# A Mamba scan whose chunk front is made over two chunks, with narrow products in column groups of TensorE

## The chip, the cores and the metric

The kernel runs on one core of a Trainium2 chip. The metric is the device time of one execution in microseconds, lower is better. The engines are named as in the profile: PE (TensorE matmuls) and PEld (its weight loads), DVE (VectorE), ACT (ScalarE), POOL (GpSimd), SP (the queue that issues DMAs). Each has its own instruction stream and they meet at semaphores only.

## What is computed

Two layers on x of 128 sequences, 64 steps and 256 features, all in fp32. The first is a linear attention with a FiLM output; the second, which takes three quarters of the time, is a Mamba block. Cut to what matters here, with the 64 steps in a permuted order:

```python
h  = layernorm(x) * (1 + scale) + shift              # [128, 64, 256]
xm, z = split(h @ W_in)                              # 512 features each
xm = silu(causal_conv(xm, conv_w, 4 taps) + conv_b)
dtr, B, C = split(xm @ W_xp, [64, 16, 16])
dt = softplus(dtr @ W_dt + b_dt)                     # [128, 64, 512]
for each step t, state s of 16:                      # A = -exp(A_log)
    hst = hst * exp(dt_t * A) + (dt_t * xm_t) * B_t
    y_t = sum_s(hst * C_t)
y = (y + xm * D) * silu(z)
out = x + gate * (y @ W_out)
```

## The kernel before

After the attention part and a setup the Mamba part works through CHUNKS = 16 chunks of T = 4 steps. It is written as *bodies*: body c scans chunk c. A body has 64 *slots* (ITEMS = 16 states x 4 steps), and in each slot i an engine does one item of the scan and whatever else is put in that slot. Items go in blocks of eight: four states, two steps.

One item on its way: ACT makes the decays exp(dt * A) of a whole block one block ahead, two `decay` activations (L632) in each slot; PE turns an item's four 128x128 decay tiles into one of four PSUM banks, two slots ahead (`turn_decay`, L527); DVE multiplies them by the state (`keep_state`, L742) and adds dt * x * B (`feed_state`, L752), two items at a time; POOL (L452), or ACT for the states 3, 7, 11 and 15 (L675, in slot i+2), multiplies the new state by C into one of eight `scaled` buffers; PE sums it into a y bank with transposing matmuls, LAG = 5 slots later (`sum_state`, L537). ACT's scaling waits for DVE's item, PE's turn waits for the item four before it, and each engine's stream is strictly in order.

The *front* of a chunk prepares its scan. In its order of data: rows are gathered by DMA into xg and modulated on POOL; PE turns them (jobs h0, h1, L575) and ACT copies them to hT; PE multiplies by W_in for x (u0 to u3, L579) and ACT copies the product to raw and makes the first tap of the convolution (L665); the other taps are on POOL (two of four feature blocks, L464 and L468) and DVE (two, L798); ACT takes tanh (L701) and DVE the silu product (L804); PE makes the low-rank input (job dtr, L584), dt (dt0 to dt3, L593) and B and C (bc, L589); ACT takes relu, abs and exp of dt (L654, L656, L670) and one Ln (L704) with a table load on either side; POOL adds them and multiplies by x (L475, L478); PE turns the product (x0 to x3, L597) and ACT copies it to dtx (L658). For z there are z0 to z3 (L570), a tanh (L708) and gates on POOL (L503, L507). Jobs out0 and out1 (L567) multiply the gated y of half a chunk by W_out; DVE scales the rows (L769) and SP stores them. Skip terms x * D are PE's L548, y's gate DVE's L761.

All products of the front share two PSUM banks in turn (`side_bank`): a job waits until the one before the last has been copied out. Which slot a job, tap, tanh or gate stands in is given by hand, by the table `SLOTS` and the numbers behind it. In the kernel before, body c makes the whole front of chunk c+1: h and u in slots 0 to 10, z in 14 to 21, dtr 22 to 25, dt 27 to 33, bc 35 to 38, x in 48 to 54. Body -1 makes chunk 0's front and scans nothing; body 15 scans and makes none.

## Time and profile before

| | |
|---|---|
| median of the runs | 2333.99 us (2333.95 to 2335.63) |
| profiled execution, its own time | 2334.89 us |
| its span, first to last instruction | 2333.1 us |
| PE / DVE / ACT / POOL busy over the span | 88% / 84% / 72% / 70% |
| attention part, from the start to about | 545 us |
| setup and first front, to the first item of the scan | 620.3 us |
| scan, to the last item | 2265 us |
| last rows, gather by permutation, final sum and store, to the end | 2333.1 us |

How to read it: a busy share says how much work an engine had, not who set the pace. In the scan the timelines show for each engine which instruction started when, how long it took, and in brackets how long the engine stood idle before it and whose result ended that. Consecutive instructions of a kind are merged into one row with their count; engines are pipelined, so the distance between two starts is shorter than the duration printed.

### The profile page before, as it was taken

How to read it: one execution, taken by the hardware profiler on the slowest of the kernel's cores; microseconds unless marked ns; L12 is line 12 of the kernel's file. 1: busy time of each engine (PE TensorE's matmuls, PEld its weight loads, DVE VectorE, ACT ScalarE, POOL GpSimd, SP SyncE). 2: the span in 40 equal slices, each digit the busy share in tenths (PEclk: the TensorE clock that was granted, in tenths of full speed). 3: DMA queues.
4: the chain of work that ended last, by engine and by line, in shares of the span. 5: the costliest groups of instructions: out<-in, count | busy, mean ns of one | idle time of the engine just before them, and what ended most of it. 6: DMA issues, size and time to landing. Idle time of an engine off the chain costs nothing. (4 is left out here: it accounts for less than half of the span.)

```text
span 2333.1 us, 44474 instructions
## 1 busy us (share of the span) xinstructions
PE 2051.4 (88%) x13497; PEld 1579.0 (68%) x13497; DVE 1969.4 (84%) x3686; ACT 1688.3 (72%) x3652; POOL 1635.2 (70%) x1800
## 2 busy tenths in 40 slices
PE   4899999995699999999999999999999999999870
PEld 3566666662467777777777777777777778777760
DVE  2788888884299898989889898989989898988983
ACT  0455555552688888898888879898888979888840
POOL 2799999985667676776767677776767677676530
PEclk8999999996699999999999999999999999999995
DMA  5122212211000000000000000000000000000218
GB/s 142 39 64 64 64 62 63 62 49 36 10 1 19 6 15 6 15 15 6 15 5 19 6 15 8 13 15 6 20 6 15 6 15 15 6 6 6 95 69 288
DMA packets 71471, 80.75 MB, mean 35 GB/s; under 512 B 12227, under 2 KB 63619, under 8 KB 69188
## 3 DMA queue, kind: packets, MB, share of 16 engines
q1 hardware_dynamic: 66052, 69.52, 9.3%
q10 hardware_dynamic: 5184, 8.39, 1.0%
q8 instruction: 112, 1.84, 0.3%
q14 instruction: 123, 1.01, 0.1%
HBM read 44.33 MB, written 33.55 MB: 33 GB/s over the span
## 5 line engine op out<-in xcount | busy, mean ns | idle before, releaser
L632 ACT ACTIVATE decay<-dtT,decay_rate 128x256 f32<-128x256 f32 x2048 | 866.5, 495 | 0.2
L527 PE MATMUL bank<-ident,decay 128*128 128x128 f32 x4096 | 622.4, 275 | 101.6 <-ACT decay L632 56.0
L537 PEld LDWEIGHTS bank<-ident,scaled 128*128 128x128 f32 x4096 | 486.2, 142 | 231.6 <-issue 193.1
L537 PE MATMUL bank<-ident,scaled 128*128 128x128 f32 x4096 | 622.8, 275 | 1.5 <-POOL scaled L452 1.4
L527 PEld LDWEIGHTS bank<-ident,decay 128*128 128x128 f32 x4096 | 471.7, 141 | 143.7 <-ACT decay L632 103.7
L452 POOL TENSOR_SCALAR scaled<-state,bc 128x512 f32<-128x512 f32 x384 | 278.2, 730 | 255.9 <-DVE state L752 209.3
L742 DVE TENSOR_TENSOR bank<-bank,state 128x512 f32<-128x512 f32 x512 | 340.8, 691 | 117.7 <-PE bank L527 111.5
L452 POOL TENSOR_SCALAR scaled<-fresh,bc 128x512 f32<-128x512 f32 x384 | 273.5, 717 | 235.0 <-DVE fresh L752 214.3
L742 DVE TENSOR_TENSOR bank<-bank,fresh 128x512 f32<-128x512 f32 x512 | 340.3, 690 | 58.9 <-PE bank L527 55.4
L752 DVE SCALAR_TENSOR_TENSOR fresh<-dtx,bc,bank 128x512 f32<-128x512 f32 x512 | 356.9, 737 | 0.0
L752 DVE SCALAR_TENSOR_TENSOR state<-dtx,bc,bank 128x512 f32<-128x512 f32 x512 | 356.8, 737 | 0.0
L1067 ACT ACTIVATE kT<-kT 128x256 f32<-128x256 f32 x64 | 26.6, 416 | 218.0 <-DVE kT L1231 218.0
L579 PE MATMUL bank<-hT,w_in 128*128 128x512 f32 x256 | 132.8, 606 | 10.5 <-ACT hT L643 10.5
L675 ACT ACTIVATE scaled<-state,bc 128x512 f32<-128x512 f32 x128 | 91.7, 716 | 59.7 <-DVE state L752 59.7
L468 POOL TENSOR_TENSOR xs<-xs,tap 128x512 f32<-128x512 f32 x96 | 129.4, 1348 | 4.3
L570 PE MATMUL bank<-hT,w_in 128*128 128x512 f32 x256 | 130.1, 594 | 1.4 <-ACT zs L641 1.4
L1003 PE MATMUL bank<-w_qv,xnT 128*128 128x512 f32 x256 | 130.8, 635 | 0.0
L567 PE MATMUL bank<-w_out,zs 128*128 128x256 f32 x512 | 126.2, 380 | 0.9 <-DVE zs L761 0.9
L798 DVE SCALAR_TENSOR_TENSOR xs<-raw,taps,xs 128x512 f32<-128x512 f32 x96 | 100.8, 1077 | 14.9 <-ACT xs L665 11.7
L993 PE MATMUL bank<-xnT,w_k 128*128 128x128 f32 x512 | 76.0, 293 | 38.1 <-ACT xnT L1086 38.1
L464 POOL TENSOR_SCALAR tap<-raw,taps 128x512 f32<-128x512 f32 x96 | 96.2, 1002 | 9.3 <-ACT xs L665 8.3
L675 ACT ACTIVATE scaled<-fresh,bc 128x512 f32<-128x512 f32 x128 | 90.8, 710 | 13.5 <-DVE fresh L752 13.4
(139 smaller groups left out, 3617.0 us busy)
## 6 DMA issues: line engine op xcount, KB each, us to landing
...
```

The costliest lines, as they stand in the source:

```text
L452: gp.tensor_scalar(dst, h, cn, 1.0, ALU.mult, ALU.mult).then_inc(s_scaled_p, 1)
L468: gp.tensor_tensor(x, x, tap[:, :], ALU.add).then_inc(s_tapadd, 1)
L527: mm = pe.transpose(dec_bank[i % DECAY_BANKS][:, m * P:(m + 1) * P], decay[:, i // BLOCK % 2, n % GROUP, m, t % HALF * P:(t % HALF + 1) * ...
L537: mm = pe.matmul(y_bank[t % HALF][:, m * P:(m + 1) * P], scaled[:, i % RING, m * P:(m + 1) * P], ident[:, :], is_transpose=True, start=Fal ...
L567: mm = pe.matmul(side[:, q * D:(q + 1) * D], zs[z][:, m, t * P:(t + 1) * P], w_out[:, m, :], start=(m == 0), stop=(m == CB - 1))
L570: mm = pe.matmul(side[:, :], w_in[:, piece, DI + k * P:DI + (k + 1) * P], hT[:, piece, :], start=(piece == 0), stop=(piece == FB - 1))
L579: mm = pe.matmul(side[:, :], w_in[:, piece, k * P:(k + 1) * P], hT[:, piece, :], start=(piece == 0), stop=(piece == FB - 1))
L632: act.activation(decay[:, block % 2, e // CB, m, :], dtT[par][:, m, half * HTOK:(half + 1) * HTOK], ACT.Exp, scale=decay_rate[:, m, n:n + ...
L675: act.activation(dst, h, ACT.Copy, scale=cn).then_inc(s_scaled_a, 1)
L742: ve.tensor_tensor(dec_bank[i % DECAY_BANKS][:, :], dec_bank[i % DECAY_BANKS][:, :], h, ALU.mult)\
L752: ve.scalar_tensor_tensor(state_of(n, t), dtx[par][:, t, :], bc[:, par, t, n:n + 1], dec_bank[i % DECAY_BANKS][:, :], ALU.mult, ALU.add).t ...
L1003: mm = pe.matmul(b_qvp[:, :], xnT[:, k % 2, c, :], w_qv[:, c, :], start=(c == 0), stop=(c == FB - 1))
```

## The change

The front of chunk k is now spread over bodies k-2 and k-1, and its last piece over body k itself. Positions in the new table count from the start of body k-2: `at(0, ...)` is body k-2, `at(B1, ...)` body k-1, `at(B2, ...)` body k, `at(B3, ...)` body k+1. There is one more body, -2, in front. Besides:

- dtr is made in two pieces of two matmuls, for two feature blocks side by side, into partitions 0 to 63 and 64 to 127 of the bank; W_dt stands twice in w_dt, so that one product over 128 rows adds the halves.
- B and C are made in a new job bcT as four matmuls into four groups of 32 partitions, copied to bcT by ACT, and turned and added up by four matmuls with `eye_sum`, four stacked 32x32 identities.
- x's tanh goes to the dt buffer of the chunk instead of tmp.

The core of the diff:

```diff
-        w_dt = sb("w_dt", [DTR, DI])
+        w_dt = sb("w_dt", [P, DI])
+        eye_sum = sb("eye_sum", [P, 2 * DS])
...
-        SLOTS = dict(zip(JOBS, ((0,), (1,), (3, 4), (5, 6), (7, 8), (9, 10), (11, 12, 13),
-                                (14, 15), (16, 17), (18, 19), (20, 21),
-                                (22, 23, 24, 25), (27,), (29,), (31,), (33,), (35, 36, 37, 38),
-                                (42, 43, 44), (48,), (50,), (52,), (54,))))
+        SLOTS = {"dtr": at(B1, 9, 13), "out1": at(B3, 10, 11, 12), "dt0": at(B1, 16), "bcT": at(B1, 17, 18),
+                 "dt1": at(B1, 20), "bc": at(B1, 22, 23), "dt2": at(B1, 25), "dt3": at(B1, 29),
+                 "z0": at(B1, 32, 33), "z1": at(B1, 34, 35), "z2": at(B1, 37, 38), "z3": at(B1, 39, 41),
+                 "out0": at(B2, 42, 43, 44), "x0": at(B1, 46), "x1": at(B1, 48), "x2": at(B1, 49), "x3": at(B1, 50),
+                 "h0": at(0, 51), "h1": at(0, 52), "u0": at(0, 53, 54), "u1": at(0, 55, 56),
+                 "u2": at(0, 57, 58), "u3": at(0, 59, 60)}
...
-        POOL_TAP_SLOT = 6
-        VECTOR_TAPS = {10: (2, 0), 12: (2, 1), 14: (2, 2), 13: (3, 0), 15: (3, 1), 16: (3, 2)}
-        X_ORDER, X_TANH, X_GATE = (0, 2, 3, 1), (13, 16, 18, 20), (15, 17, 19, 21)
-        MODULATE, CARRY, SOFTPLUS, GATES = (28, 33), 24, 38, 56
+        POOL_TAP_SLOTS = at(57, *range(2 * len(POOL_TAPS)))
+        VECTOR_TAPS = [(2, 0), (3, 0), (2, 1), (3, 1), (2, 2), (3, 2)]
+        VECTOR_TAP_SLOTS = at(62, *range(len(VECTOR_TAPS)))
+        X_ORDER, X_TANH, X_GATE = (0, 2, 3, 1), at(B1, 1, 4, 5, 8), at(B1, 3, 6, 7, 10)
+        MODULATE, CARRY, LN = at(0, 21, 25), B1 + 18, B1 + 31
+        SOFTPLUS = at(B1, *range(33, 33 + 2 * CB))
+        Z_TANH, Z_GATES = B1 + 52, at(B2, 5, 6, 8, 9, 11, 12, 14, 15)
...
-                    pe.wait_ge(s_xs, (c + 1) * CB + piece + 1)
-                    m = X_ORDER[piece]
-                    mm = pe.matmul(side[0:DTR, :], w_xp[:, m, 0:DTR], xs[1 - par][:, m, :],
-                                   start=(piece == 0), stop=(piece == CB - 1))
+                    pe.wait_ge(s_xs, k * CB + 2 * piece + 2)
+                    for g in range(P // DTR):
+                        m = X_ORDER[2 * piece + g]
+                        mm = pe.matmul(side[g * DTR:(g + 1) * DTR, :], w_xp[:, m, 0:DTR], x[:, m, :],
+                                       start=(piece == 0), stop=(piece == pieces - 1), skip_group_check=True)
+                elif kind == "bcT":
+                    for g in (2 * piece, 2 * piece + 1):
+                        mm = pe.matmul(side[g * 2 * DS:(g + 1) * 2 * DS, :], w_xp[:, g, DTR:DTR + 2 * DS],
+                                       x[:, g, :], start=True, stop=True, tile_position=(0, g * 2 * DS))
                 elif kind == "bc":
-                    t = piece
-                    for m in range(CB):
-                        mm = pe.matmul(side[:, t * 2 * DS:(t + 1) * 2 * DS], xs[1 - par][:, m, t * P:(t + 1) * P],
-                                       w_xp[:, m, DTR:DTR + 2 * DS], start=(m == 0), stop=(m == CB - 1))
+                    if piece == 0:
+                        moved(pe, k, "bcT")
+                    for t in (2 * piece, 2 * piece + 1):
+                        mm = pe.matmul(side[:, t * 2 * DS:(t + 1) * 2 * DS], bcT[:, t * P:(t + 1) * P], eye_sum[:, :],
+                                       start=True, stop=True)
...
-                        if i == X_TANH[0]:
-                            reached(act, s_zs, (c + 1) * CB)
-                        act.activation(tmp[:, m, :], xs[1 - par][:, m, :], ACT.Tanh, scale=0.5).then_inc(s_xtanh, 1)
+                if step == 0:
+                    reached(act, s_decay, (k - 1) * BLOCKS * GROUP * CB)
+                act.activation(dtT[k % 2][:, m, :], xs[k % 2][:, m, :], ACT.Tanh, scale=0.5).then_inc(s_xtanh, 1)
...
+                    for g in range(P // DTR):
+                        sp.dma_start(w_dt[g * DTR:(g + 1) * DTR, :], W_dt).then_inc(s_ssm_w, 16)
```

How the instructions stand, at three places of a body in mid-run. First ACT around the Ln, before (slots 32 to 37; L654 to L670 is the dt group, L632 a decay, L704 the Ln):

```order
L654 ACTIVATE dtT0<-bank6,col 128x512
L656 ACTIVATE tmp<-bank6,col 128x512
L670 ACTIVATE tmp<-tmp 128x512
L632 ACTIVATE decay<-dtT1,decay_rate 128x256 x2
L704 ACT_TABLE_LOAD
L704 ACTIVATE tmp<-tmp 128x2048
L632 ACT_TABLE_LOAD
L632 ACTIVATE decay<-dtT1,decay_rate 128x256 x4
L675 ACTIVATE scaled<-fresh,bc 128x512
```

The same on ACT in the changed kernel, slots 30 to 36 (L648 is the decay, L674 to L691 the dt group, L715 the Ln, L696 the scaling, L657 z's copy):

```order
L674 ACTIVATE dtT0<-bank6,col 128x512
L677 ACTIVATE tmp<-bank6,col 128x512
L691 ACTIVATE tmp<-tmp 128x512
L648 ACTIVATE decay<-dtT1,decay_rate 128x256 x2
L715 ACT_TABLE_LOAD
L715 ACTIVATE tmp<-tmp 128x2048
L648 ACT_TABLE_LOAD
L648 ACTIVATE decay<-dtT1,decay_rate 128x256 x4
L696 ACTIVATE scaled<-state,bc 128x512
L648 ACTIVATE decay<-dtT1,decay_rate 128x256 x2
L657 ACTIVATE zs0<-bank7 128x512
```

The Ln moved from slot 35 to slot 31, and z's copies now follow it.

Second, ACT around z's tanh, before (slots 54 to 58; L658 copies x to dtx, L708 is z's tanh):

```order
L658 ACTIVATE dtx0<-bank7 128x512
L632 ACTIVATE decay<-dtT1,decay_rate 128x256 x4
L658 ACTIVATE dtx0<-bank6 128x512
L708 ACTIVATE tmp<-zs0 128x2048
L632 ACTIVATE decay<-dtT0,decay_rate 128x256 x4
L675 ACTIVATE scaled<-state,bc 128x512
```

And in the changed kernel, slots 50 to 55 (L679 the copy to dtx, L659 the copy of h to hT, L722 z's tanh, L663 the copy of u):

```order
L679 ACTIVATE dtx0<-bank6 128x512
L648 ACTIVATE decay<-dtT1,decay_rate 128x256 x2
L679 ACTIVATE dtx0<-bank7 128x512
L648 ACTIVATE decay<-dtT1,decay_rate 128x256 x2
L659 ACTIVATE hT<-bank6 128x512
L722 ACTIVATE tmp<-zs0 128x2048
L648 ACTIVATE decay<-dtT1,decay_rate 128x256 x2
L696 ACTIVATE scaled<-fresh,bc 128x512
L659 ACTIVATE hT<-bank7 128x512
L648 ACTIVATE decay<-dtT1,decay_rate 128x256 x4
L663 ACTIVATE raw<-bank6 128x512
```

The next chunk's h copies have come to stand around z's tanh, with the u copies behind them; before, they were at the start of the next body.

Third, DVE where the taps are, in the changed kernel, slots 62 to 3 (L822 a tap, L829 the gate of x, L782 and L792 keep and feed, L801 the gate of y). Before, taps and gates of x stood between the items of slots 10 to 21:

```order
L822 SCALAR_TENSOR_TENSOR xs0<-raw,taps,xs0 128x512 x2
L782 TENSOR_TENSOR bank2<-bank2,state 128x512
L782 TENSOR_TENSOR bank3<-bank3,state 128x512
L792 SCALAR_TENSOR_TENSOR fresh<-dtx1,bc,bank2 128x512
L792 SCALAR_TENSOR_TENSOR fresh<-dtx1,bc,bank3 128x512
L822 SCALAR_TENSOR_TENSOR xs0<-raw,taps,xs0 128x512 x2
L782 TENSOR_TENSOR bank4<-bank4,state 128x512
L782 TENSOR_TENSOR bank5<-bank5,state 128x512
L801 TENSOR_TENSOR zs0<-bank0,zs0 128x4x128
L792 SCALAR_TENSOR_TENSOR fresh<-dtx1,bc,bank4 128x512
L792 SCALAR_TENSOR_TENSOR fresh<-dtx1,bc,bank5 128x512
L822 SCALAR_TENSOR_TENSOR xs0<-raw,taps,xs0 128x512 x2
```

All six taps now stand with four items, from the end of one body into the next.

## Rows read from the trace of the kernel before

**Rows 1.** Windows by stage: length, busy time (count) of each engine, clock, DMA.

```profile
core 0: us, PE busy (x) PEld busy (x) DVE busy (x) ACT busy (x) POOL busy (x), PEclk, DMA share, GB/s
620.00:2182.00 1562.00, 1469.40 (x10186) 1172.73 (x10184) 1419.25 (x2160) 1341.90 (x2772) 1108.92 (x1186) 1.00 0.03 11
2182.00:2266.00 84.00, 69.60 (x565) 63.56 (x564) 82.84 (x133) 54.96 (x126) 37.51 (x53) 1.00 0.27 107
```

**Rows 2.** Timeline of DVE: start us, duration us, what, count.

```profile
1286.12 1.28 DVE L742 TENSOR_TENSOR bank<-bank,fresh 128x512 f32<-128x512 f32 x2
1287.31 1.39 DVE L752 SCALAR_TENSOR_TENSOR state<-dtx,bc,bank 128x512 f32<-128x512 f32 x2
1288.63 1.28 DVE L742 TENSOR_TENSOR bank<-bank,state 128x512 f32<-128x512 f32 x2
```

**Rows 3.** Timeline of ACT around dt, the Ln and a u copy.

```profile
1298.56 0.71 ACT L675 ACTIVATE scaled<-fresh,bc 128x512 f32<-128x512 f32 x1
1299.17 0.90 ACT L632 ACTIVATE decay<-dtT,decay_rate 128x256 f32<-128x256 f32 x2
1299.97 0.67 ACT L654 ACTIVATE dtT<-bank,col 128x512 f32<-128x512 f32 x1
...
1301.78 1.69 ACT L632 ACTIVATE decay<-dtT,decay_rate 128x256 f32<-128x256 f32 x4
...
1309.21 0.89 ACT L632 ACTIVATE decay<-dtT,decay_rate 128x256 f32<-128x256 f32 x2
...
1314.64 1.71 ACT L632 ACTIVATE decay<-dtT,decay_rate 128x256 f32<-128x256 f32 x4
...
1357.63 0.60 ACT L647 ACTIVATE raw<-bank 128x512 f32<-128x512 f32 x1 [0.90 <-PE bank L579]
...
1358.98 1.69 ACT L632 ACTIVATE decay<-dtT,decay_rate 128x256 f32<-128x256 f32 x4
```

**Rows 4.** Groups by line: busy us, mean ns | idle before us.

```profile
L798 DVE SCALAR_TENSOR_TENSOR xs<-raw,taps,xs 128x512 f32<-128x512 f32 x96 | 100.8, 1077 | 14.9 <-ACT xs L665 11.7 <-DVE yo L769 3.0
L804 DVE SCALAR_TENSOR_TENSOR xs<-tmp,xs 128x512 f32<-128x512 f32 x64 | 49.2, 770 | 2.5 <-ACT tmp L701 2.5
L761 DVE TENSOR_TENSOR zs<-bank,zs 128x512 f32<-128x512 f32 x64 | 43.5, 679 | 0.9 <-PE bank L537 0.9
L708 ACT ACTIVATE tmp<-zs 128x2048 f32<-128x2048 f32 x16 | 30.6, 1914 | 0.5
```

**Rows 5.** Timeline of PE: a z slot (L570), then a slot of dtr (L584).

```profile
1283.96 1.02 PE L570 MATMUL bank<-hT,w_in 128*128 128x512 f32 x2
1284.82 0.60 PE L537 MATMUL bank<-ident,scaled 128*128 128x128 f32 x4
1285.26 0.60 PE L527 MATMUL bank<-ident,decay 128*128 128x128 f32 x4
1285.79 1.07 PE L584 MATMUL bank<-xs,w_xp 128*64 128x512 f32 x2
1286.79 0.66 PE L537 MATMUL bank<-ident,scaled 128*128 128x128 f32 x4
```

**Rows 6.** Timeline of PE behind the Ln.

```profile
1316.40 0.66 PE L527 MATMUL bank<-ident,decay 128*128 128x128 f32 x4 [1.55 <-ACT decay L632]
```

**Rows 7.** Timeline of PE in the attention part, a product into two column groups.

```profile
301.46 0.66 PE L1012 MATMUL bank<-attnT,kq 128*64 128x128 f32 x8
302.05 0.44 PE L1022 MATMUL bank<-ident,kT 128*128 128x128 f32 x2
```

**Rows 8.** Windows around falls of the granted clock; columns as in rows 1.

```profile
519.00:520.00 1.00, 0.00 (x0) 0.00 (x0) 1.00 (x5) 0.90 (x3) 0.92 (x2) 0.89 0.11 38
583.00:584.00 1.00, 0.00 (x0) 0.00 (x0) 1.00 (x1) 0.20 (x1) 1.00 (x2) 1.00 0.00 0
585.00:586.00 1.00, 0.95 (x2) 0.00 (x0) 0.00 (x0) 0.02 (x1) 1.00 (x1) 0.50 0.00 0
598.00:600.00 2.00, 2.00 (x11) 2.00 (x11) 0.00 (x0) 1.39 (x1) 0.53 (x1) 0.50 0.00 0
```

**Rows 9.** Timeline of PE in the first front: the u products.

```profile
560.51 8.91 PE L579 MATMUL bank<-hT,w_in 128*128 128x512 f32 x16 [0.78 <-ACT hT L643]
```

More of the change, by code:

```diff
@@ new lines, in build, with chunk_at @@
+        ROWS = {"out1": B3 + 12, "out0": B2 + 44}
+        BODIES = range(-2, CHUNKS + 1)
+        def chunk_at(c, i, position):
+            k = c + 2 - position // ITEMS
+            return k if position % ITEMS == i and 0 <= k < CHUNKS else None
+        SEQUENCE, COMPLETED = {}, {}
+        for c in BODIES:
+            for i in range(ITEMS):
+                for job in SLOTS:
+                    first, last = chunk_at(c, i, SLOTS[job][0]), chunk_at(c, i, SLOTS[job][-1])
+                    if first is not None:
+                        SEQUENCE[job, first] = len(SEQUENCE)
+                    if last is not None:
+                        COMPLETED[job, last] = len(COMPLETED)
@@ L399, in prefetch_resid @@
                         .then_inc(s_fin_r, 16)
-            def body(c, par, post, scan, pre):
-                if pre and c + 2 < CHUNKS:
-                    filled(sp, c, "h1")
-                    apart(sp)
-                    gather(c + 2)
-                if post:
+            for c in BODIES:
+                if scanned(c - 1):
                     store_rows(c - 1, 1)
@@ L517, in mamba_tensor @@
+            for c in BODIES:
+                for i in range(ITEMS):
+                    slot(c, i)
         def mamba_tensor(pe):
@@ L618, in mamba_tensor, with slot @@
-            mamba_bodies(pe, body)
+            SKIPS = [index_of(0, t) + LAG - 1 for t in range(T)]
+            def slot(c, i):
+                if i + 2 < ITEMS:
+                    if scanned(c):
+                        turn_decay(c, i + 2)
+                elif scanned(c + 1):
+                    turn_decay(c + 1, i + 2 - ITEMS)
+                if scanned(c) and i in SKIPS:
+                    skip_term(c, SKIPS.index(i))
+                for job in SLOTS:
+                    for piece, position in enumerate(SLOTS[job]):
+                        k = chunk_at(c, i, position)
+                        if k is not None:
+                            fill(k, job, piece)
+                if i >= LAG and scanned(c):
+                    sum_state(c, i - LAG)
+                if i < LAG and scanned(c - 1):
+                    sum_state(c - 1, i - LAG + ITEMS)
@@ L717, in mamba_scalar @@
+            for c in BODIES:
+                for i in range(ITEMS):
+                    slot(c, i)
             final_rows(act, 1)
```

460 lines of the change are left out of this document (228 added, 232 removed).

## The prediction, made before the changed kernel was run

> **What bounds the kernel now.** First the windows by stage. From 620 to 2182 us, the fifteen bodies that scan one chunk and prepare the next, DVE is busy 1419 of 1562 us, PE 1469, ACT 1342, POOL 1109; one body takes 1562 / 15 = 104.1 us. The last body only scans: 84 us, DVE busy 83 [rows 1]. So no engine fills the 104 us: four engines with 74 to 98 us of work each wait for one another in turn.
>
> Then the timelines, for what a step costs from start to start. DVE: two items (two L742, two L752) take from 1286.12 to 1288.63, 2.51 us, 1.26 an item [rows 2]; a tap (L798) has 1.08 mean, about 1.0 to the next start, L804 and L761 under 0.8 [rows 4]. With 64 items 80.3, six taps 6, four gates of x 2.6, four of y 2.4 and two L769 about 2, DVE needs 93 of the 104, so 11 us of a body are waits. ACT: a scaling (L675) 0.61, two decays 0.80, a dt group (L654, L656, L670) 1.81; from the two decays before the Ln to the decay after it 5.43, less 0.80 is 4.63, both table loads in it; a u copy with its first tap 1.35 [rows 3]; z's tanh 1.91 [rows 4]. That makes 88. PE: a z or u piece 0.86, the four transposes of a sum or of a turn 0.44, so an item 0.87, and a slot of the low-rank input 1.00 [rows 5]; an out slot has six records of half a z record's 0.43, 1.3. That makes 94. PE's longest wait in a steady body is 1.55 us, for decays behind the Ln [rows 6], and the granted clock stays 1.00, the upper of its two levels (2.4 GHz; 0.50 is 1.2 GHz) [rows 1].
>
> What a reader is to see: today PE's dense slots (u, out1, z, dtr in 3 to 25) stand beside DVE's heavy ones (taps and gates in 10 to 21), and where ACT is heaviest (dt and Ln in 28 to 35) PE has dt and then bc. Heavy places that coincide share their cost.
>
> **The change, part by part.**
>
> *Column groups.* dtr's four pieces at 1.00 become two pieces of two matmuls in different halves of the columns. That such pairs run together shows in the attention part: L1012's eight records of 128 columns go into both halves, and the next work starts 0.59 us later [rows 7], where eight at a quarter of 0.43 would take 0.86. So 4.0 becomes 2.0. B and C: 32 short records, 3.4 us at that same 0.107, become two paired pieces bcT, 2.0, and eight short records, 0.9. w_dt over 128 rows instead of 64 saves at most a tiling change, 1.00 - 0.86 = 0.14, in each of four slots. PE gains 2.0 + 0.5 + 0.6 = 3.1 a body if pairs overlap; if they don't, it loses 0.3. The Trainium skill (TensorEngine Tiling, Key Properties) says that a change of tiling mode drains the engine; by the row a drain costs 0.14, and as four slots before and four after have it, it changes nothing in the sum.
>
> *ACT* gets one more 128x512 copy (bcT), 0.5. DVE and POOL keep their instructions. x's tanh in the dt buffer takes away its wait for z's gates, which before had ended long before it: worth nothing by itself, it only allows z's gates to stand later.
>
> *The order* is what counts. By blocks of eight slots, with the prices above, DVE / ACT / PE. Before: 11.3/11.3/13.1, 16.6/10.8/15.7, 12.8/11.2/14.2, 10.1/11.8/12.2, 11.3/16.0/12.4, 11.2/7.6/11.4, 10.1/11.5/8.7, 10.1/7.6/7.0; the largest of each add up to 105, where 104 is measured. After: 17.0/9.2/7.9, 11.5/8.7/13.4, 10.1/11.8/11.6, 10.1/16.0/8.7, 11.3/9.1/14.0, 11.2/8.6/12.7, 10.1/13.3/11.8, 12.0/11.7/11.3; that is 110. Less work on PE, but the heavy places no longer coincide. How much neighbouring blocks lend each other is seen by following the ring of waits through one body. ACT cannot run ahead: its scaling in slot i waits for DVE's item i-2. Take 0 as the end of item 15 on DVE, which ACT's scaling in slot 17 waits for.
> 1. ACT from there to its scaling in slot 33: 32 decays 12.8, five scalings 3.1, four dt groups 7.2, bcT and bc 0.7, Ln 4.6, waits for the fills of dt0 and bcT 1.2: 29.6. PE's sum in slot 36 needs this scaling. PE is there by 26.2 (its turns follow DVE: 22 items at 1.26, a y gate, less the items by which it leads), so it idles about 3.5 us, and DVE's item 39 comes at 30.8 instead of 29.4.
> 2. PE from that sum to the fill of x0 in slot 46: sums and turns of ten slots 9.1, four z pieces 3.5, a skip term 0.9, out0 3.5, a wait for z0's copy 0.4: 17.4, so 47.1. ACT is at its slot 47 by 44.6 and waits 2.5.
> 3. ACT from x0's copy to h1's in slot 53: six copies 3.0, twelve decays 4.8, two scalings 1.2, z's tanh 1.9, handing over 0.2: 11.1, so 58.2. z's tanh now stands ahead of h1's copy, and PE, at slot 53's u piece by 55.3, waits 3 us for it.
> 4. PE: that piece and its sum 1.3, seven slots of 1.73, the turn that item 63 needs 0.7, handing over 0.1: 14.2, so 72.4.
> 5. DVE ends item 63 at 74.4; then 16 items 20.1, all six taps 6, gates 2.6 and 1.2, L769 0.9: 30.8, so 105.2 at item 15 of the next body.
> So 105.2 against 104.1. What PE gains ends as its idle time: 3.5 and 3 us at these two places and some 9 in slots 1 to 8, where DVE is heavy and PE has only turns and sums.
>
> *The clock.* PE does nothing from 583 to 584 with the granted clock still at 1.00, and has 0.50 at 585; in the second from 519 without work on PE the clock falls likewise, to a mean of 0.89; and at 598 to 600, PE busy all the time, it is still 0.50 [rows 8]. The cheapest low stretch is at the start of the Mamba part: sixteen u records take 8.91 us [rows 9], where 16 at 0.43 are 6.9, so 2.0 are lost. One such stretch behind the 3.5 us of step 1 falls on step 2, all of which is on the ring: 107.2 a body. Behind step 3 as well: 109.2. The Trainium skill (TensorE: Matmul & The Clock Gate, HAM oscillation) says that matmul bursts with idle stretches between them start at half clock each time, which would be the 109.2. The trace agrees at 585; the 1.55 us gaps of a body did not do it.
>
> *The ends.* Chunk 1's h and u now stand ahead of the first scan: eight u matmuls had 8.91 us in the same empty place [rows 9], and DVE's taps of chunk 1, ahead of its first item, wait for the last copy: +12 (8 to 20), with decays ready by then taken off. Body 14 has no h and u, its last slots run at DVE's pace: -8. Together +4. The second load of w_dt and the sum over ident hide beside the attention part; if they didn't, under 1 us each.
>
> The sum is made on the profiled execution: span 2333.1, plus 15 x (107.2 - 104.1), plus 4, is 2383.6. The median of the runs, 2334.0, is 0.9 above that span: **2384**. With no low stretch it is 2354, with two 2414.
>
> **Rivals.**
> *The ring closes shorter (faster).* If PE never holds ACT or DVE in steps 2 and 4, what remains is ACT from slot 17 to the last u copy in slot 61 (88 decays 35.2, twelve scalings 7.3, dt 7.2, Ln 4.6, tanh 1.9, copies 5.7, u 5.4: 67.3) and DVE from there, 29.8: 97.1 a body. It decides at slot 46, by whether x0 is filled 2.5 us earlier, and at slot 53. For it: PE has 91 us of work, and dt and the Ln are ten slots earlier, so nothing is late for the scan. Halfway, 100.1 a body: 2334 - 60 + 4, 2278. Against it: steps 1 to 5 are orders of instructions.
> *A long low clock.* As from 585 to 600, where dense work did not bring it back: 4 to 7 us more on steps 2 and 4, 111 to 114 a body, 2441 to 2486. For it: PE idle for 9 of 17 us in slots 1 to 8, ahead of dense slots 9 to 18.
> *Nothing gained.* The blocks lend each other a little more than I allow, 103.8 a body: 2333.
> *Pairs do not overlap.* 3.4 more on PE, of which the dtr and bcT slots in 9 to 18 put 2 on DVE's path: 2414 with one low stretch, inside the forecast.
>
> **How the numbers follow.** Ring as walked, with none, one or two short low stretches, 2343 to 2415: 0.48. Long low clock, above 2415: 0.17. Shorter ring, below 2329: 0.27. No change that can be told: 0.08; a measurement tells about 0.2%, 4.7 us, from none. So slower 0.65, same 0.08, faster 0.27. The forecast's own range is 2343 to 2415; for 8 in 10 I leave out the lower part of the faster case and the upper part of the long clock: 2285 to 2445.
>
> **What would show it.** Right: once a body PE waits 3 us or more for ACT's scaling behind the Ln, and again for hT behind z's tanh; PE busy near half the time in slots 1 to 8; granted clock under 1.00 in windows of a body; bodies of 105 to 109 us; two w_xp slots of 1.0 for dtr. Wrong: bodies under 104, no wait of PE over 2 us, a clock of 1.00; then the failing step is the one of 1 or 3 where the wait is missing.

## The result and the profile after

| | before | after |
|---|---|---|
| median of the runs | 2334.81 us (2333.95 to 2338.54) | 2406.66 us (2406.57 to 2409.8) |
| span of the profiled execution | 2333.1 us | 2408.1 us |
| first item of the scan on DVE | 620.30 us | 634.40 us |
| one body, mean of fourteen | 103.91 us | 108.81 us |

The changed kernel is slower: ratio 1.0308, 95% interval 1.029 to 1.0326. That is 72 us where 50 were forecast, inside the range, and on the side that had 0.65.

A body is read from one place of DVE's order to the same place one chunk on; out0's rows serve here (L769 of before, L809 of after). Timeline of DVE, before, first and last of fifteen such rows: 1454.76 us over fourteen bodies, 103.91 each.

```profile
704.78 0.68 DVE L769 TENSOR_TENSOR yo<-bank,mod_gate 128x512 f32<-128x512 f32 x1
...
2159.54 0.68 DVE L769 TENSOR_TENSOR yo<-bank,mod_gate 128x512 f32<-128x512 f32 x1
```

The same of after: 1523.30 us, 108.81 each. Of these fourteen, eleven take 109.0 us, one 109.3 and two 107.35, as the one that the two rows in the middle bound.

```profile
708.52 0.69 DVE L809 TENSOR_TENSOR yo<-bank,mod_gate 128x512 f32<-128x512 f32 x1 [1.03 <-PE bank L571]
...
1797.39 0.69 DVE L809 TENSOR_TENSOR yo<-bank,mod_gate 128x512 f32<-128x512 f32 x1 [1.03 <-PE bank L571]
...
1904.74 0.69 DVE L809 TENSOR_TENSOR yo<-bank,mod_gate 128x512 f32<-128x512 f32 x1 [1.03 <-PE bank L571]
...
2231.82 0.69 DVE L809 TENSOR_TENSOR yo<-bank,mod_gate 128x512 f32<-128x512 f32 x1 [1.03 <-PE bank L571]
```

So 1523.30 - 1454.76 = 68.5 of the 75.0 us between the two spans come from the bodies; what lies before the first and behind the last of these rows makes the other 6.5.

Windows of the kernel after, over the stretch of [rows 1]: PE 1469 us before, now 1381; DVE 1419, now 1376. Less work got done in the same time, and the clock is no longer 1.00.

```profile
620.00:2182.00 1562.00, 1381.32 (x9420) 1117.79 (x9420) 1375.84 (x2051) 1271.23 (x2651) 1066.24 (x1132) 0.96 0.03 10
```

One body cut at the ring's five steps (its zero, the end of item 15 on DVE, is at 1206.9 us; columns as in rows 1):

```profile
1206.90:1237.60 30.70, 29.92 (x211) 22.94 (x208) 29.23 (x48) 30.12 (x59) 23.23 (x25) 1.00 0.01 1
1237.60:1254.10 16.50, 16.35 (x110) 13.68 (x111) 12.37 (x20) 13.76 (x33) 11.29 (x13) 1.00 0.03 11
1254.10:1265.10 11.00, 8.31 (x78) 8.10 (x75) 11.00 (x19) 10.96 (x22) 4.12 (x7) 1.00 0.12 35
1265.10:1282.80 17.70, 17.70 (x100) 12.87 (x101) 10.84 (x17) 14.11 (x30) 8.90 (x12) 0.90 0.06 16
1282.80:1316.20 33.40, 24.64 (x175) 21.03 (x174) 33.19 (x46) 19.73 (x46) 26.70 (x26) 0.95 0.02 9
```

The busy engine changes from line to line as the ring said: PE and ACT in the first, PE in the second, ACT in the third while PE stands still (DVE is busy there too, but it waits 2.46 us for PE right behind), PE in the fourth, DVE in the fifth while PE has 25 of 33 us of work. The steps end at 30.7, 47.2, 58.2, 75.9 and 109.3, where 30.8, 47.1, 58.2, 74.4 and 105.2 were forecast. This is the body of 109.3 us; in those of 109.0 step 5 is 33.1 long and not 33.4.

Step 3 on ACT (timeline): z's tanh at 1261.15 stands ahead of h1's copy at 1264.37.

```profile
1260.68 0.58 ACT L659 ACTIVATE hT<-bank 128x512 f32<-128x512 f32 x1
1261.15 1.91 ACT L722 ACTIVATE tmp<-zs 128x2048 f32<-128x2048 f32 x1
1262.96 0.91 ACT L648 ACTIVATE decay<-dtT,decay_rate 128x256 f32<-128x256 f32 x2
1263.75 0.72 ACT L696 ACTIVATE scaled<-fresh,bc 128x512 f32<-128x512 f32 x1
1264.37 0.59 ACT L659 ACTIVATE hT<-bank 128x512 f32<-128x512 f32 x1
```

And on PE (timeline): 2.69 us idle, then the second u piece takes 1.87 us and the third 1.02. The last two rows are the two longest idle times around the turn to the next body.

```profile
1265.10 1.14 PE L583 MATMUL bank<-hT,w_in 128*128 128x512 f32 x2 [2.69 <-ACT hT L659]
...
1267.74 1.87 PE L583 MATMUL bank<-hT,w_in 128*128 128x512 f32 x2
...
1270.32 1.02 PE L583 MATMUL bank<-hT,w_in 128*128 128x512 f32 x2
...
1287.42 0.63 PE L531 MATMUL bank<-ident,decay 128*128 128x128 f32 x4 [2.60 <-DVE fresh L792]
...
1292.96 0.76 PE L531 MATMUL bank<-ident,decay 128*128 128x128 f32 x4 [3.61 <-DVE fresh L792]
```

Twelve of the fourteen handovers look like that. The other two, those of the two short bodies, have the same idle time and keep the clock. Over six microseconds from 1.5 us behind the start of u0 the granted clock is, handover by handover: 1.00, then falling almost steadily over nine of them from 0.83 to 0.72, then 1.00, then 0.83, 0.82, 0.80. So the low stretch moves against the handover from body to body until it misses it once; the length of the idle time alone does not decide. Windows right behind the handover, an ordinary one and one of the two:

```profile
1157.00:1163.00 6.00, 6.00 (x29) 4.34 (x28) 2.22 (x4) 2.87 (x7) 0.00 (x0) 0.73 0.12 32
1811.00:1817.00 6.00, 6.00 (x36) 4.10 (x35) 3.32 (x5) 4.55 (x11) 1.36 (x3) 1.00 0.16 47
```

PE gets 29 instead of 36 instructions done in 6 us, and the body is 109.0 - 107.35 = 1.7 us longer: the price of one low stretch on the ring, read without any experiment. Another one, from 1293 to 1297, lies in step 5, in which DVE waits once, for 0.21 us; it costs nothing.

Step 5, DVE (timeline): a pair of taps takes 2.5 us from its start to that of the next work, where [rows 4] let me count 2.0.

```profile
1282.84 2.58 DVE L822 SCALAR_TENSOR_TENSOR xs<-raw,taps,xs 128x512 f32<-128x512 f32 x2
1285.34 1.28 DVE L782 TENSOR_TENSOR bank<-bank,state 128x512 f32<-128x512 f32 x2
1286.54 1.39 DVE L792 SCALAR_TENSOR_TENSOR fresh<-dtx,bc,bank 128x512 f32<-128x512 f32 x2
1287.85 2.52 DVE L822 SCALAR_TENSOR_TENSOR xs<-raw,taps,xs 128x512 f32<-128x512 f32 x2
```

POOL in the same time (timeline): its own tap additions, 1.7 us beside a DVE tap, 1.27 without one.

```profile
1283.16 1.71 POOL L463 TENSOR_TENSOR xs<-xs,tap 128x512 f32<-128x512 f32 x1
...
1288.12 1.70 POOL L463 TENSOR_TENSOR xs<-xs,tap 128x512 f32<-128x512 f32 x1
```

The groups by line say the same for the whole run; [rows 4] has 1077 and 770 ns for these two.

```profile
L822 DVE SCALAR_TENSOR_TENSOR xs<-raw,taps,xs 128x512 f32<-128x512 f32 x96 | 122.3, 1312 | 61.1 <-ACT xs L686 61.0
L829 DVE SCALAR_TENSOR_TENSOR xs<-dtT,xs 128x512 f32<-128x512 f32 x64 | 61.8, 985 | 1.8 <-ACT dtT L710 1.8
```

The column groups do what they should. A slot of dtr (timeline of PE) now holds two products in 1.01 us, what one took in [rows 5]:

```profile
1304.00 1.08 PE L589 MATMUL bank<-xs,w_xp 128*64 128x512 f32 x4
1305.01 0.66 PE L541 MATMUL bank<-ident,scaled 128*128 128x128 f32 x4
```

### The profile page after: what moved, and what is told of

Same layout as the page of the kernel before. It is cut to its first block and busy times, and to the rows that moved or that the text cites. A ratio compares the mean times of both kernels' runs of the same rounds, so it can differ in the third digit from the quotient of the medians.

```text
span 2408.1 us, 44027 instructions
## 1 busy us (share of the span) xinstructions
PE 2026.9 (84%) x13241; PEld 1575.7 (65%) x13241; DVE 1996.0 (83%) x3687; ACT 1683.6 (70%) x3668; POOL 1636.8 (68%) x1800
## 3 DMA queue, kind: packets, MB, share of 16 engines
q14 instruction: 123, 1.01, 0.1%
## 5 line engine op out<-in xcount | busy, mean ns | idle before, releaser
L648 ACT ACTIVATE decay<-dtT,decay_rate 128x256 f32<-128x256 f32 x2048 | 869.7, 497 | 0.2
L531 PE MATMUL bank<-ident,decay 128*128 128x128 f32 x4096 | 635.0, 279 | 156.0 <-DVE fresh L792 94.8
L541 PEld LDWEIGHTS bank<-ident,scaled 128*128 128x128 f32 x4096 | 501.2, 144 | 226.7 <-issue 174.2
L541 PE MATMUL bank<-ident,scaled 128*128 128x128 f32 x4096 | 631.3, 278 | 2.9 <-POOL scaled L447 1.2
L531 PEld LDWEIGHTS bank<-ident,decay 128*128 128x128 f32 x4096 | 485.4, 144 | 184.8 <-ACT decay L648 114.0
L782 DVE TENSOR_TENSOR bank<-bank,state 128x512 f32<-128x512 f32 x512 | 336.6, 693 | 92.6 <-PE bank L531 92.6
L782 DVE TENSOR_TENSOR bank<-bank,fresh 128x512 f32<-128x512 f32 x512 | 341.0, 695 | 72.0 <-PE bank L531 69.0
L792 DVE SCALAR_TENSOR_TENSOR fresh<-dtx,bc,bank 128x512 f32<-128x512 f32 x512 | 358.0, 742 | 0.0
L792 DVE SCALAR_TENSOR_TENSOR state<-dtx,bc,bank 128x512 f32<-128x512 f32 x512 | 358.0, 742 | 0.0
L583 PE MATMUL bank<-hT,w_in 128*128 128x512 f32 x256 | 144.4, 658 | 42.4 <-ACT hT L659 42.4
L822 DVE SCALAR_TENSOR_TENSOR xs<-raw,taps,xs 128x512 f32<-128x512 f32 x96 | 122.3, 1312 | 61.1 <-ACT xs L686 61.0
L463 POOL TENSOR_TENSOR xs<-xs,tap 128x512 f32<-128x512 f32 x96 | 142.4, 1483 | 0.8
L574 PE MATMUL bank<-hT,w_in 128*128 128x512 f32 x256 | 131.9, 601 | 5.7 <-ACT zs L657 5.2
L696 ACT ACTIVATE scaled<-fresh,bc 128x512 f32<-128x512 f32 x128 | 91.5, 715 | 52.2 <-DVE fresh L792 50.4
L710 ACT ACTIVATE dtT<-xs 128x512 f32<-128x512 f32 x64 | 39.8, 622 | 116.6 <-DVE xs L822 90.3
L470 POOL TENSOR_TENSOR dtT<-dtT,tmp 128x512 f32<-128x512 f32 x64 | 82.3, 1286 | 40.9 <-ACT tmp L715 40.9
```

The costliest lines, as they stand in the source:

```text
L463: gp.tensor_tensor(x, x, tap[:, :], ALU.add).then_inc(s_tapadd, 1)
L531: mm = pe.transpose(dec_bank[i % DECAY_BANKS][:, m * P:(m + 1) * P], decay[:, i // BLOCK % 2, n % GROUP, m, t % HALF * P:(t % HALF + 1) * ...
L541: mm = pe.matmul(y_bank[t % HALF][:, m * P:(m + 1) * P], scaled[:, i % RING, m * P:(m + 1) * P], ident[:, :], is_transpose=True, start=Fal ...
L574: mm = pe.matmul(side[:, :], w_in[:, piece, DI + b * P:DI + (b + 1) * P], hT[:, piece, :], start=(piece == 0), stop=(piece == FB - 1))
L583: mm = pe.matmul(side[:, :], w_in[:, piece, b * P:(b + 1) * P], hT[:, piece, :], start=(piece == 0), stop=(piece == FB - 1))
L648: act.activation(decay[:, block % 2, e // CB, m, :], dtT[c % 2][:, m, half * HTOK:(half + 1) * HTOK], ACT.Exp, scale=decay_rate[:, m, n:n ...
```

## The experiments

Three causes are in question: the handover at h1 with its low clock, the taps beside POOL's, and behind both the placing of the work. Against them stands that the bodies are long wherever the jobs stand, because the front's chain is. All kernels ran beside the kernel before; its medians were 2336.06, 2335.98 and 2334.4 us in the three sets. Body means are worked out from out0's rows as above.

| kernel | median, us | against before | body, us |
|---|---|---|---|
| after | 2406.66 | 1.0308 (1.029 to 1.0326) | 108.8 |
| a1_tanh_later | 2361.09 | 1.011 (1.0093 to 1.0126) | 105.6 |
| a2_small_pool_taps | 2360.90 | 1.0108 (1.0092 to 1.0125) | 105.9 |
| a4_filler | 2391.08 | 1.0238 (1.0221 to 1.0256) | 107.4 |
| a5_both | 2324.82 | 0.996 (0.9946 to 0.9974) | 103.5 |
| a3_no_columns | 2434.37 | 1.0442 (1.039 to 1.0494) | 110.6 |
| b1_columns_only | 2370.67 | 1.0154 (1.0137 to 1.0171) | 106.1 |
| b2_columns_early | 2365.59 | 1.0122 (1.0105 to 1.0139) | 105.8 |
| b3_filler | 2340.52 | 1.0024 (1.0014 to 1.0034) | 103.9 |
| v1_spread | 2210.73 | 0.9467 (0.9451 to 0.9482) | 95.7 |
| v2_spread | 2243.01 | 0.9601 (0.9585 to 0.9617) | 97.7 |
| v1_no_columns | 2251.63 | 0.9644 (0.9628 to 0.9661) | 98.1 |
| v4_spread | 2212.08 | 0.9476 (0.9461 to 0.9492) | 95.5 |

### The handover at h1

```diff
-        Z_TANH, Z_GATES = B1 + 52, at(B2, 5, 6, 8, 9, 11, 12, 14, 15)
+        Z_TANH, Z_GATES = B1 + 53, at(B2, 5, 6, 8, 9, 11, 12, 14, 15)
```

> The changed kernel with one number changed: ScalarE's tanh of z is issued one slot later, behind the copy of h1 instead of ahead of it. Theory A (the handover at h1 is on the ring and brings the low clock): TensorE's wait for hT, 42.4 us over 16 bodies, falls below 10, the low-clock stretch right behind it goes (1.7 us a body, the difference between the bodies of 109.0 and of 107.35 us), and the body falls from 109.0 to 104.9 to 106.5 us: 2345 to 2372 us in all. Rival (TensorE is saturated in slots 33 to 62 and the wait only moves to the next operation): within 8 us of 2407.

2361.09 us, in theory A's range. A row of PE's timeline and the window behind it (columns as in rows 1): the wait is 0.90 us and the clock 1.00. It is shorter, not gone: over the whole run PE still waits 16.2 us for hT, where theory A said less than 10.

```profile
1245.00 1.10 PE L583 MATMUL bank<-hT,w_in 128*128 128x512 f32 x2 [0.90 <-ACT hT L659]
```
```profile
1246.00:1252.00 6.00, 6.00 (x39) 4.42 (x38) 4.44 (x7) 5.97 (x13) 2.38 (x4) 1.00 0.23 66
```

One slot for one activation is worth 3.2 us a body. How much of that is the clock alone, a filler tells:

```diff
                     if piece == 0:
+                        if b == 0:
+                            for g in range(24):
+                                pe.transpose(side[:, g % 4 * P:(g % 4 + 1) * P], ident[:, :], ident[:, :])
                         moved(pe, k, "h1")
```

> The changed kernel with 24 spare transposes of the identity (2.6 us at the 0.109 us that each takes at full clock) on TensorE in front of its wait for the copies of h, into the bank that u0 is about to fill; nothing else moves. They fill the 2.7 us in which TensorE stands still and add nothing behind it. Theory A (the low clock behind the handover is brought by the idle time, and costs 1.7 us in the bodies of 109.0 us): granted clock 1.00 behind u0, bodies of 107.3 us, 2380 to 2388 us. Rival (the clock falls there anyway, or costs nothing): 2400 to 2412 us.

Bodies of 107.4 us and a clock of 1.00 behind u0, as theory A says; the median, 2391, is 3 us above its range and 9 below the rival's. The window behind u0, which starts at 1149.08 here (columns as in rows 1), to be compared with the ordinary one above, 0.73:

```profile
1150.00:1156.00 6.00, 6.00 (x38) 4.37 (x37) 3.31 (x5) 4.62 (x10) 1.57 (x3) 1.00 0.11 35
```

Useless work in the gap makes every body like the two short ones. So of the 3.2 us, 1.4 are the clock (1.7 in twelve bodies of fourteen) and 1.8 the wait.

### The taps beside POOL's

```diff
-                    gp.tensor_scalar(tap[:, :], raw[:, m, j * P:j * P + TOK], taps[:, m, j:j + 1], 1.0,
+                    gp.tensor_scalar(tap[:, 0:8], raw[:, m, j * P:j * P + 8], taps[:, m, j:j + 1], 1.0,
...
-                    gp.tensor_tensor(x, x, tap[:, :], ALU.add).then_inc(s_tapadd, 1)
+                    gp.tensor_tensor(x[:, 0:8], x[:, 0:8], tap[:, 0:8], ALU.add).then_inc(s_tapadd, 1)
```

> The changed kernel with GpSimd's six convolution taps of a chunk done on 8 of 512 columns only (the rest of those taps is left out of the result); all orders and waits stay. Theory A (VectorE's taps in slots 62 to 67 are stretched by GpSimd's taps beside them): the mean of VectorE's taps falls from 1312 ns to below 1000, step 5 of the ring from 33.4 to about 31, the body by 2 to 3 us: 2362 to 2379 us. Rival (the taps would take 1.2 us each anyway, the stretch comes from their own operands): the mean stays above 1200 ns and the time within 8 us of 2407.

2360.90 us, a microsecond better than theory A's range. With POOL's taps out of the way (groups by line) DVE's take 798 ns instead of 1312, a pair 1.5 instead of 2.5 us:

```profile
L822 DVE SCALAR_TENSOR_TENSOR xs<-raw,taps,xs 128x512 f32<-128x512 f32 x96 | 72.9, 798 | 63.1 <-ACT xs L686 63.1
```

The body falls by 3.0 us, which looks like the whole of the taps' 6 x 0.51, but is not. Nine of its fourteen bodies take 105.3 us and five 106.8: against bodies with the same clock (107.35 and 109.0) that is 2.0 and 2.2 less. The other 0.9 comes from the clock, which now stays up in nine bodies and not in two, behind the same idle time of 2.69 us. Windows behind u0, one of either kind (columns as in rows 1):

```profile
1245.00:1251.00 6.00, 6.00 (x38) 4.32 (x37) 3.31 (x5) 4.55 (x10) 1.52 (x3) 1.00 0.10 32
1350.00:1356.00 6.00, 6.00 (x29) 3.84 (x28) 2.02 (x4) 3.11 (x8) 0.18 (x1) 0.80 0.16 45
```

And of the 3.1 us that the taps give back, the gates of x take some 0.8: their mean grows from 985 to 1182 ns, as they now meet POOL's gates of z.

The items beside the taps (L782, L792) keep their 0.69 and 0.74 us in both kernels: they have one operand in PSUM, the taps and the gates of x have both in SBUF. The Trainium skill (SBUF — State Buffer, Who interferes with whom) has that as a rule: a VectorE instruction with two SBUF inputs contends with a GpSimd one that reads SBUF, and the contention is an exclusive lock. The trace agrees, on which instructions suffer and on how. The mean of a pair, 1.25 us, hides it; narrower timelines keep the two taps of the pair at 1282.84 apart:

```profile
1282.84 0.89 DVE L822 SCALAR_TENSOR_TENSOR xs<-raw,taps,xs 128x512 f32<-128x512 f32 x1
1283.65 1.76 DVE L822 SCALAR_TENSOR_TENSOR xs<-raw,taps,xs 128x512 f32<-128x512 f32 x1
```

POOL's addition starts at 1283.16 and takes 1.71 us. The first tap ends at 1283.73; with 1.27 us, the addition's time alone, that makes 1285.0, and it ends at 1284.87. The second tap starts at 1283.65, does not end before the addition does, and is done 0.54 us behind it, at 1285.41. So the three go nearly one behind the other, and the pair takes 2.5 us.

Both edits of these two sections together:

> The changed kernel with the edits of a1_tanh_later and a2_small_pool_taps together (GpSimd's taps on 8 of 512 columns, the rest of them left out of the result). Each alone took 46 us off 2407. Theory A (the handover at h and the taps' contention stand behind each other on one ring and add up): 2310 to 2328 us. Rival (they cover one another, so that the second is worth little once the first is gone): 2340 to 2361 us.

2324.82 us, in theory A's range: the second edit is worth 36 us after the first, 46 alone, since alone it also keeps the clock up in seven more bodies. Between bodies with the same clock the effects add up: 2.0 us for the taps (107.35 to 105.3, 105.6 to 103.5), 1.8 for the tanh (107.35 to 105.6, 105.3 to 103.5). With both, a body is 103.5 us, 0.4 below the kernel before, so the two places are worth more than the 4.9 us that the bodies had lost. That nothing is left over for the front's longer way is not shown by it: the edit takes all of POOL's taps away, and in the kernel before they already stretch DVE's, to a mean of 1077 ns [rows 4] against 798 without them, 1.7 us a body; and PE has less to do than there, by the column groups.

### What the column groups are worth

```diff
                     for g in range(P // DTR):
                         m = X_ORDER[2 * piece + g]
-                        mm = pe.matmul(side[g * DTR:(g + 1) * DTR, :], w_xp[:, m, 0:DTR], x[:, m, :],
+                        mm = pe.matmul(side[0:DTR, :], w_xp[:, m, 0:DTR], x[:, m, :],
...
-                    for t in (2 * piece, 2 * piece + 1):
-                        mm = pe.matmul(side[:, t * 2 * DS:(t + 1) * 2 * DS], bcT[:, t * P:(t + 1) * P], eye_sum[:, :],
+                    for t in (2 * piece, 2 * piece + 1):
+                        for m in range(CB):
+                            mm = pe.matmul(side[:, t * 2 * DS:(t + 1) * 2 * DS], x[:, m, t * P:(t + 1) * P],
```

> The changed kernel without the column groups: dt's low-rank input by four matmuls into 64 partitions, B and C by sixteen matmuls from x directly, no bcT job, w_dt on 64 partitions; the front's other positions stay. TensorE gets 3.1 us more of side work in a body, in slots 9 to 23. Theory A (VectorE is the bound in these slots, TensorE is level with it): half of it or less shows, 2407 to 2430 us. Rival (TensorE runs behind from slot 9 on, so all of it is on the path): 2440 to 2455 us.

2434.37 us, between the two ranges and 4 us above theory A's, and its four runs lie further apart than any others here (2430 to 2454). Bodies of 110.6, so 1.8 of the 3.1 us show in the mean; but the clock behind u0 falls in six handovers only. Between bodies with the same clock (109.6 against 107.35) it is 2.3. Slots 9 to 23 had less room than I gave them.

The same part alone, in the order of before:

```diff
-                                (22, 23, 24, 25), (27,), (29,), (31,), (33,), (35, 36, 37, 38),
+                                (23, 25), (27,), (29,), (31,), (33,), (34, 35), (37, 38),
```

> The kernel before with the column groups alone: dtr in two pairs of matmuls in slots 23 and 25, bcT in 34 and 35, bc in 37 and 38, the front otherwise as before. TensorE's side work falls by 3.1 us a body in slots 22 to 38. Theory A (what the column groups save counts where TensorE is the bound, which it is in most of these slots of the kernel before): a body of 101.5 to 103 us, 2290 to 2320 us. Rival (the extra handover of bcT through ScalarE costs what the matmuls save): 2325 to 2345 us.

Both theories are wrong: 2370.67 us, 35 slower than before, with less work on PE. A row of PE's timeline, rows of ACT's, and a window around them (columns as in rows 1) tell why:

```profile
1221.29 1.03 PE L597 MATMUL bank<-eye_sum,bcT 128*128 128x32 f32 x4 [5.27 <-ACT bcT L659]
```
```profile
1216.53 1.91 ACT L714 ACTIVATE tmp<-tmp 128x2048 f32<-128x2048 f32 x1
...
1219.76 0.91 ACT L640 ACTIVATE decay<-dtT,decay_rate 128x256 f32<-128x256 f32 x2
1220.57 0.58 ACT L659 ACTIVATE bcT<-bank 128x512 f32<-128x512 f32 x1
```
```profile
1217.00:1225.00 8.00, 3.71 (x18) 3.74 (x19) 2.36 (x4) 7.31 (x14) 3.18 (x3) 0.60 0.01 2
```

bcT's copy stands behind the Ln, PE idles 5.27 us, and the clock (last line, 0.60) is down when PE has work again. The first repair is to take bcT away from there:

```diff
-                                (23, 25), (27,), (29,), (31,), (33,), (34, 35), (37, 38),
+                                (22, 23), (25, 26), (27,), (29,), (31,), (33,), (35, 37),
```

> The kernel before with the column groups alone, as b1_columns_only, but bcT in slots 25 and 26, so that its copy stands far ahead of the logarithm on ScalarE and not right behind it: dtr in 22 and 23, bc in 35 and 37. Theory A (b1 lost its time to the 5.3 us in which TensorE waited for bcT's copy behind the logarithm, and to the low clock that followed): no wait for bcT, no low clock, and the 3.1 us of TensorE's work come back in part: bodies of 102 to 103.9 us, 2300 to 2334 us. Rival (one more handover and one more copy cost more than the matmuls save, wherever they stand): 2340 us and more.

2365.59 us, the rival's range. But it is not the handover. The wait for bcT is gone and another one stands in its place, as a row of PE's timeline and the window around it show: where the kernel before idled 1.55 us behind the Ln [rows 6], PE, now 3 us ahead, idles 4.80.

```profile
1225.76 1.12 PE L529 MATMUL bank<-ident,decay 128*128 128x128 f32 x4 [4.80 <-ACT decay L640]
```
```profile
1223.00:1231.00 8.00, 5.25 (x25) 5.25 (x26) 1.90 (x4) 7.99 (x19) 6.12 (x6) 0.57 0.00 0
```

ACT sets the pace there, so faster matmuls only lengthen PE's idle time, and that brings the low clock. If so, useless work must repair it:

```diff
+                reached(pe, s_state, c * ITEMS + i + 1 - DECAY_BANKS)
+                if i == 42:
+                    for g in range(40):
+                        pe.transpose(dec_bank[i % DECAY_BANKS][:, g % 4 * P:(g % 4 + 1) * P], ident[:, :], ident[:, :])
                 pe.wait_ge(s_decay, (c * BLOCKS + i // BLOCK) * GROUP * CB + n % GROUP * CB + CB)
-                reached(pe, s_state, c * ITEMS + i + 1 - DECAY_BANKS)
```

> b2_columns_early with 40 spare transposes of the identity (4.4 us at 0.109 us each) on TensorE in each chunk, in front of its wait for the decays of item 42, where it stood still for 4.8 us, into the bank that this turn is about to fill. The body keeps the wait, the filler only covers it; in the last chunk, where there was no such wait, it costs up to 4.4 us once. Theory A (the low clock behind that idle time is what makes b2's body of 105.9 us longer than the 103.9 of the kernel before): clock 1.00, bodies of 103.9 to 104.4 us, 2338 to 2350 us. Rival (ScalarE's chain behind the logarithm alone sets it): bodies of 105.5 us or more, 2360 us and more.

2340.52 us, theory A: 25 us faster by 40 spare transposes a chunk, bodies of 103.9 as before. Of the 6 us that are left against the kernel before, 4.3 are the last chunk, where the filler covers no wait. The window around the turn of item 42, which starts at 1212.06 here (columns as in rows 1), has the clock back:

```profile
1209.00:1217.00 8.00, 7.17 (x59) 6.60 (x58) 3.42 (x6) 7.99 (x18) 6.61 (x7) 1.00 0.01 2
```

So in the order of before the column groups are worth nothing, and cost 2 us a body through the clock (105.8 against 103.9).

### Placing

v1_spread keeps every instruction of the changed kernel and moves the jobs. Of its table, the lines that matter, in the notation of after:

```diff
-                 "z0": at(B1, 32, 33), "z1": at(B1, 34, 35), "z2": at(B1, 37, 38), "z3": at(B1, 39, 41),
-                 "h0": at(0, 51), "h1": at(0, 52), "u0": at(0, 53, 54), "u1": at(0, 55, 56),
-                 "u2": at(0, 57, 58), "u3": at(0, 59, 60)}
-        VECTOR_TAP_SLOTS = at(62, *range(len(VECTOR_TAPS)))
-        Z_TANH, Z_GATES = B1 + 52, at(B2, 5, 6, 8, 9, 11, 12, 14, 15)
+                 "z0": at(B1, 19, 26), "z1": at(B1, 34, 35), "z2": at(B1, 36, 38), "z3": at(B1, 37, 39),
+                 "h0": at(0, 43), "h1": at(0, 44), "u0": at(0, 52, 55), "u1": at(0, 56, 57),
+                 "u2": at(B1, 0, 1), "u3": at(B1, 4, 5)}
+        VECTOR_TAP_SLOTS = at(B1, 5, 7, 7, 7, 7, 11)
+        Z_TANH, Z_GATES = B2 + 8, at(B2, 9, 11, 15, 16, 17, 19, 23, 26)
```

> The changed kernel's instructions, all of them, with another table of positions: h in slots 43 and 44 of the first body and u0, u1 in 52 to 57, u2, u3 one body on in 0 to 5, VectorE's taps in 5 to 11, dtr in 11 and 15, bcT in 22 and 24, z spread over 19 to 39, out0 in 47 to 50, x in 58 to 61, the tanh of z in 8 of the last body. Theory A (what the changed kernel loses is placement: TensorE's side work stands packed where VectorE waits for it, and VectorE's taps where TensorE waits for them): the body comes down towards the busier engine's own time, 96.6 us for TensorE and 96.0 for VectorE in a body of 109.0, so to 95 to 99 us: 2205 to 2275 us. Rival (the chain of handovers of the front and the low clock set the body, wherever the jobs stand): 2330 us or more.

2210.73 us, theory A's range: 8% below the changed kernel and 5.3% below the one before. The window from 700 to 2100 us (columns as in rows 1) has DVE busy for 97% and PE for 96%, with the clock at 1.00; DVE's taps take 0.88 us in the mean.

```profile
700.00:2100.00 1400.00, 1344.08 (x9701) 1108.35 (x9699) 1354.57 (x2111) 1289.13 (x2697) 1065.83 (x1146) 1.00 0.04 14
```

Of the kernel before, the same stretch, with DVE at 91% and 103.9 us a body:

```profile
700.00:2100.00 1400.00, 1319.00 (x9176) 1055.89 (x9175) 1275.16 (x1944) 1202.28 (x2483) 999.61 (x1070) 1.00 0.04 11
```

The Trainium skill (Perfetto Trace Analysis, Optimization Strategy) advises to interleave the regimes of a kernel in which different engines are the busiest. The trace agrees: that, and no instruction less, is 13 us a body here.

```diff
-                 "h0": at(0, 51), "h1": at(0, 52), "u0": at(0, 53, 54), "u1": at(0, 55, 56),
-        VECTOR_TAP_SLOTS = at(62, *range(len(VECTOR_TAPS)))
+                 "h0": at(0, 42), "h1": at(0, 48), "u0": at(0, 51, 53), "u1": at(0, 52, 54),
+        VECTOR_TAP_SLOTS = at(B1, -2, 3, 0, 2, 2, 5)
```

> As v1_spread, with yet another table: h in slots 42 and 48, u0 to u3 in 51 to 63, VectorE's taps in 62 to 69, dtr in 6 and 14, bcT in 20 and 22, z over 23 to 41, out0 in 46 to 49, x in 55 to 61, the tanh of z in 4 of the last body. Theory A: bodies of 96 to 100 us, 2220 to 2290 us. Rival as for v1_spread: 2330 us or more.

2243.01 us with bodies of 97.7, theory A as well; the clock is 0.98 over the scan, so some of its idle times are still long.

A third table of that kind:

```diff
-                 "h0": at(0, 51), "h1": at(0, 52), "u0": at(0, 53, 54), "u1": at(0, 55, 56),
-        VECTOR_TAP_SLOTS = at(62, *range(len(VECTOR_TAPS)))
+                 "h0": at(0, 42), "h1": at(0, 46), "u0": at(0, 49, 51), "u1": at(0, 54, 55),
+        VECTOR_TAP_SLOTS = at(B1, 5, 6, 6, 7, 7, 7)
```

> The changed kernel's instructions with a third table in the manner of v1_spread: h in slots 42 and 46, u0 and u1 in 49 to 55, u2 and u3 in 63 to 69, GpSimd's taps from 49 on, VectorE's in 5 to 7, dtr in 13 and 15, bcT in 21 and 24, z spread over 14 to 41, x in 57 to 61. Theory A (VectorE's own work, 92.0 us in a body of v1_spread's 95.7, is the floor, and the 3.7 us above it are waits that another order can take away in part): bodies of 93.5 to 95.7 us, 2185 to 2211 us. Rival (the waits only move, and the front's longer chain brings others): 2211 to 2250 us.

2212.08 us with bodies of 95.5: the time is 1 us inside the rival's range, the bodies are in theory A's, so it stands on the border of the two. Against v1_spread nothing is gained. DVE is no busier (1350.67 of 1400 us), the waits only moved, and the first rows come 8 us later.

The column groups once more, where PE is nearly full; the edit is that of a3_no_columns, on v1_spread's table:

> v1_spread without the column groups: dt's low-rank input by four matmuls into 64 partitions in the two slots of before, B and C by sixteen matmuls from x in the two slots of bc, no bcT. 3.1 us more of TensorE's work in a body, 1.2 us less of it and of ScalarE's in the bcT job counted in. Theory A (in v1_spread TensorE is busy for 95% of the time, so what the column groups save shows): a body of 97.5 to 98.9 us against 95.7, 2236 to 2258 us. Rival (VectorE, busy for 96%, is the bound, and TensorE has the room): 2205 to 2225 us.

2251.63 us, theory A, 41 slower than with them. The clock is 1.00 in both, so the 2.4 us a body (98.1 against 95.7) are PE's work itself, and without them the spread front over two bodies is worth 103.9 - 98.1 = 5.8 us a body against the kernel before. PE's timeline shows one of its two dtr slots, 1.9 us long, against 1.0 in pairs:

```profile
1143.63 1.93 PE L603 MATMUL bank<-xs,w_xp 128*64 128x512 f32 x4
```

## Why the prediction came out as it did

**Right: the walk around the ring.** Steps 1 to 3 were forecast at 30.8, 47.1 and 58.2 and came at 30.7, 47.2 and 58.2; ACT waited 2.79 us for x0 (2.5), PE 2.69 for hT (3); from 1284 to 1302, around slots 1 to 8, PE was busy for 9.5 of 18 us, the half that was forecast. The wait that a1_tanh_later cuts from 2.69 to 0.90 us was named, with its cause. Even the table by blocks of eight slots, crude as it is, gave 110 and 105 for bodies of 109.0 and 103.9.

**Right: pairs overlap.** 1.01 and 0.99 us a slot, so that rival is out. That PE's gain would end as idle time is what b2_columns_early shows in the order of before; in that of after 2.3 of 3.1 us did count, clock for clock (a3_no_columns).

**Wrong in place: the idle time in slot 36.** Step 1 said that PE stands still for 3.5 us there. Its longest wait in that stretch is 0.64 us, and it is busy for 29.92 of the 30.70: it was itself late with its dt and z pieces, which "PE is there by 26.2" left out. The step's end was right all the same, since ACT, busy for 30.12, sets it.

**Wrong in place, right in size: the low clock.** One short stretch a body was forecast behind step 1, for 2.0 us. It came behind step 3, in twelve of fourteen bodies, for 1.7. a4_filler shows that the idle time brings it. The long low clock did not come: PE was back at 1.00 within 6 us each time. The forecast for two low stretches on the ring was 109.2 a body, and 109.0 were measured; that is chance, since only one lies on the ring, and the rest is step 5.

**Mis-sized: step 5.** It was put at 30.8 us and took 33.1 (33.4 in the body shown). The term is the six taps: 6 us by a mean of before, and 7.5 here. That mean was no price of a tap but a mixture: one alone takes 0.75 us, as a2_small_pool_taps shows, a pair with POOL's work beside it 2.5, and in the new order all three pairs are of the second kind. The gates of x, now beside POOL's gates of z, grew from 770 to 985 ns in the mean, which is 0.9 more. This is 2.3 us a body, and all of what the forecast lacks: 105.2 + 2.3 would be 107.5 with no low clock, where 107.35 was measured.

**The ends.** +12 for the first item was +14.1; +4 for both ends together was +6.5. The sum took 3.1 us for fifteen bodies; it was 4.9 for fourteen.

**The shorter ring** (2278) needed x0 2.5 us earlier or no wait in slot 53. Neither came by itself. Its "halfway" of 100.1 was also mis-added: between 97.1 and 105.2 lies 101.2, which would have been 2294. But v1_spread goes below the 97.1 us that I gave as the floor of its two chains: I had taken ACT's and DVE's places for fixed. The change's two-body front makes such tables possible; its own table did not use them.

**Open.** What sets whether one of several equal idle times brings the low clock (twelve of fourteen here, five of fourteen in a2_small_pool_taps, six of fourteen in a3_no_columns); the pattern says when it falls, no run shows why. A shorter form of z's tanh or of the Ln was not tried, nor were the gates of x apart from POOL's gates by themselves. And no run spread the jobs of the kernel before, so how much of the way to 2211 us needs the front over two bodies is not shown.
